# A two-layer graph network on one core: a support stage one pair deeper without GpSimd, two adj sums beside layer 0, z ahead of a low half

## What is computed

```python
h = jnp.maximum(_layernorm(x), 0.0)
# layer 0: quantised graph convolution
w_norm = (weight - mean) / std
weight_q = _weight_quant(w_norm, wgt_alpha, 3)      # round(|clip(w/alpha)| * 7) / 7 * sign * alpha
xq = _act_quant(h, act_alpha, 4)                    # round(min(h/alpha, 1) * 15) / 15 * alpha
support = relu(xq @ weight_q)
support_q = _act_quant(support, act_alpha2, 4)
x = x + adj @ support_q
# layer 1
h = jnp.maximum(_layernorm(x), 0.0)
S = (adj + adj.T) * 0.5 + I
dinv = where(deg > 0, deg ** -0.5, 0)               # deg = row sums of S
x = x + adj @ ((dinv[:, None] * S * dinv[None, :]) @ h)
```

## Time and profile before

| what | us |
|---|---|
| median of 3 runs (541.35 to 542.11) | 541.65 |
| the profiled execution, its own time | 541.03 |
| its span, first to last instruction | 538.9 |
| PE busy | 507.5 (94%) |
| DVE busy | 299.9 (56%) |
| ACT busy | 160.9 (30%) |
| POOL busy | 18.1 (3%) |

### The profile page before, as it was taken

One profiled execution on the slowest core, in us unless ns is written; L12 is line 12 of the kernel. 1 busy time (PEld: TensorE's weight loads), 2 busy tenths in 40 slices (PEclk: granted clock), 3 DMA queues, 4 the chain that ended last, 5 costly groups with the idle time before them and its releaser, 6 DMA issues.

```text
span 538.9 us, 6658 instructions
## 1 busy us (share of the span) xinstructions
PE 507.5 (94%) x2520; PEld 252.1 (47%) x2520; DVE 299.9 (56%) x415; ACT 160.9 (30%) x222; POOL 18.1 (3%) x24
## 2 busy tenths in 40 slices
PE   2868899999999979999998999999999999999997
PEld 2745455555555424444433444444444444444443
DVE  4996399997677996887789777743010010010001
ACT  0687576444444224434324212213000000000000
POOL 0134200000000000000000000000000000000000
PEclk9999999999999989999998999999999999999999
DMA  6970170254435132232322332204510000001001
GB/s 239 402 296 2 47 226 0 58 173 146 152 118 174 44 115 78 78 117 78 118 78 78 118 109 86 78 0 140 192 39 20 19 34 25 19 19 39 19 19 39
DMA packets 19251, 51.64 MB, mean 96 GB/s; under 512 B 2336, under 2 KB 2336, under 8 KB 19232
## 3 DMA queue, kind: packets, MB, share of 16 engines
q1 hardware_dynamic: 18656, 51.39, 28.2%
q10 hardware_dynamic: 576, 0.00, 0.1%
HBM read 42.99 MB, written 8.39 MB: 95 GB/s over the span
## 4 chain that ended last, share of the span: by engine, by line
PE 87%; DVE 8%; ACT 2%; DMA 2%; issue 1%; SPq 0%; ACTq 0%; DVEq 0%
PE ps_a L918 31%; PE ps_p L813 17%; PE ps_p L881 7%; PE ps_a L881 7%; PE ps_b L881 7%; PE ps_m L881 4%; PE ps_h L881 3%; PE ps_a L800 3%; PE ps_b L800 2%; PE ps_b L777 2%; DMA feat<-in_x 2%; DVE st L494 1%; DVE a_in L693 1%; DVE split L702 1%; DVE a_in L692 1%
## 5 line engine op out<-in xcount | busy, mean ns | idle before, releaser
L813 PE MATMUL ps_p<-small,at 128*128 128x512 f16 x448 | 101.6, 379 | 0.0
L749 DVE SCALAR_TENSOR_TENSOR feat<-ps_a,feat 128x512 f32<-128x512 f32 x16 | 11.1, 691 | 153.8 <-PE ps_a L918 153.8
L918 PE MATMUL ps_a<-a_in,at 128*128 128x512 f16 x384 | 85.5, 379 | 0.0
L918 PE MATMUL ps_a<-small,at 128*128 128x512 f16 x384 | 85.5, 379 | 0.0
L431 ACT ACTIVATE split<-a_in 128x1024 f16<-128x1024 f32 x32 | 33.8, 1057 | 113.8 <-PE ps_p L881 60.3
L813 PEld LDWEIGHTS ps_p<-small,at 128*128 128x128 f16 x448 | 43.7, 98 | 46.4 <-POOL small L306 0.3
L702 DVE TENSOR_TENSOR split<-a_in,split 128x1024 f16<-128x1024 f32 x32 | 39.2, 1224 | 36.7 <-ACT split L431 36.7
L918 PEld LDWEIGHTS ps_a<-small,at 128*128 (+1 forms) x384 | 37.5, 98 | 45.4
L918 PEld LDWEIGHTS ps_a<-a_in,at 128*128 (+1 forms) x384 | 37.5, 98 | 45.4
L881 PE MATMUL ps_a<-feat,split 128*128 (+1 forms) x180 | 45.0, 387 | 3.2 <-DVE small L706 3.2
L881 PE MATMUL ps_p<-feat,split 128*128 (+1 forms) x180 | 45.1, 388 | 0.0
(11 more groups left out here) (139 smaller groups left out, 466.9 us busy)
## 6 DMA issues: line engine op xcount, KB each, us to landing
a_in<-in_adj SPq DMA_DIRECT2D x48, 512.0 KB, 3.7
out<-feat SPq DMA_DIRECT2D x32, 256.0 KB, 2.0
feat<-in_x SPq DMA_DIRECT2D x8, 512.0 KB, 10.5
split<-in_adj SPq DMA_DIRECT2D x8, 512.0 KB, 5.3
at<-in_adj SPq DMA_DIRECT2D x8, 512.0 KB, 16.8
feat<-out SPq DMA_DIRECT2D x4, 1024.0 KB, 9.3
at<-in_L_gnn_weight SPq DMA_DIRECT2D x2, 512.0 KB, 5.9
scal<-in_L_gnn_act_alpha ACTq DMA_DIRECT2D x2, 0.5 KB, 6.9
```

What stands on the lines that cost most here:

```text
L749: nc.vector.scalar_tensor_tensor(xr, BANK[t % 2], 1.0 / (SA * SZ), xr, ALU.mult, ALU.add)\
L813: last = nc.tensor.matmul(l0_bank(r), at_block(r, lo, j), small[:, j * D:(j + 1) * D], start=(j == 0 and lo == 0), stop=(j == T - 1 and lo ...
L918: last = nc.tensor.matmul(BANK[n], at_block(t, lo, j), z_part(j, z_lo), start=(j == 0 and lo + z_lo == 0), stop=(j == T - 1 and lo == 1))
```

## The change

Support stage: PE transposes pair 1 before it multiplies pair 0, and so on, one pair deeper; the products of a pair go to one pair of banks, `ps_b` and `ps_a` in turn, and ACT evicts them in one operation. DVE rounds in one pass (adds the constant and subtracts it) straight to f16, and the clip of the support is a pass of its own on f16; POOL has no part any more. The quantised h is held negative and offset, so that ACT's eviction of the transposes can clip it. `GROUPS` gets one group more. Fewer `keep_warm` products. ACT evicts all transposes. Only units 0 and 1 are turned in the support stage, into `ps_p`, units 2 and 3 within row 0, and 4 to 11 in rows 1 to 3 (`TURNS`). In a later row the second turn comes after 8 products, not 16.

Boundary: adj units 0 and 1 of the sweep are loaded early into `split` and `tmp` and summed and split in rows 8 to 11 of layer 0. The statistics of rows 13 to 15 come as one group. The first sweep unit takes its banks in the order 0, 1, 2, 3, 6, 7, 4, 5. In the first sweep `sum_unit(v + 1)` stands ahead of `sum_lo(v)`. Between the sweeps seven of eight z halves stand ahead of the halves of unit 17.

```diff
-RING = 6
-EARLY = 6
-AHEAD = 14
+RING = 4
+AHEAD = 12
-GROUPS = (0, 2, 6, 10, T)
-LATE_GROUPS = (0, 13, 15, T)
+GROUPS = (0, 2, 4, 8, 12, T)
+LATE_GROUPS = (0, 13, T)
+LATE_SUMS = (0, 1, 2, 3)
...
         def turn_bank(u):
-            return ps_a if u < EARLY or u % 2 == 0 else ps_b
+            return ps_p if u < 2 else ps_b if u % 2 == 0 else ps_a
         def turn_before(u):
-            return u if u <= EARLY else u - 1
+            return 0 if u in (0, 2) else u - 1 if u > 3 else 1 if u == 1 else 0
...
         def sum_in(v):
-            k = SLOT[v % 4]
+            if v == 0:
+                return splitf[:, W:2 * W]
+            if v == 1:
+                return tmp[:, :]
+            k = (v - 2) % 4
             return a_in[:, k * W:(k + 1) * W]
...
+        TURNS = {r: [2 * r + 4, 2 * r + 5] for r in range(4, T - 2)}
+        TURNS.update({1: [4, 5, 6], 2: [7, 8], 3: [9, 10, 11]})
...
-            for u in range(AHEAD):
+            for n in range(4):
+                load_x(n)
+            rows(0)
+            rows(1)
+            for n in range(4, T // 2):
+                load_x(n)
+            for u in range(2, AHEAD):
                 rows(u)
+            sums(0)
+            sums(1)
...
             def copy_transposes(m):
...
-                nc.scalar.activation(hT[m % 2], hT_ps_bank[m % 2], ACT.Copy).then_inc(hT_ready, 1)
+                nc.scalar.activation(hT[m % 2], hT_ps_bank[m % 2], ACT.Relu, scale=-1.0).then_inc(hT_ready, 1)
             def scale_support(m):
-                for t in (2 * m, 2 * m + 1):
-                    act.wait_ge(sup_ps, t + 1)
...
+                nc.scalar.activation(sq[m % 2], sup_banks(m)[:, :], ACT.Relu, scale=c_sup).then_inc(sup_out, 1)
...
+            copy_transposes(1)
+            normalise(2)
+            scale_support(0)
+            hi_turned(0)
+            normalise(3)
+            copy_transposes(2)
+            group_root(3)
+            scale_support(1)
+            hi_turned(1)
+            copy_transposes(3)
+            for n in range(4, T // 2):
+                if n == 5:
+                    group_root(4)
+                normalise(n)
+                scale_support(n - 2)
+                copy_transposes(n)
...
             def quantise(n):
...
-                nc.vector.tensor_scalar(xq[n % 2], xq[n % 2], float(ACT_LEVELS), MAGIC, ALU.min, ALU.add)\
-                  .then_inc(xq_ready, 1)
+                nc.vector.tensor_scalar(hq[n % 2], xq[n % 2], -(MAGIC + ACT_LEVELS), MAGIC, ALU.add, ALU.add)\
+                  .then_inc(hq_ready, 1)
+            def round_support(m):
+                dve.wait_ge(sup_out, m + 1)
+                nc.vector.tensor_scalar(small[:, 2 * m * D:2 * (m + 1) * D], sq[m % 2], MAGIC, -MAGIC,
+                                        ALU.add, ALU.add).then_inc(sup_rounded, 1)
             def clip_support(m):
...
+                dve.wait_ge(sup_rounded, m + 1)
+                both = small[:, 2 * m * D:2 * (m + 1) * D]
+                nc.vector.tensor_scalar(both, both, float(ACT_LEVELS), None, ALU.min).then_inc(sq_ready, 1)
...
+            for r in range(1, 14):
+                now = TURNS[r]
+                turned_out(now[0])
+                x1_tile(r - 1)
+                for u in now[1:]:
+                    turned_out(u)
+                if r - 4 in LATE_SUMS:
+                    column_sum_late(r - 4)
+                if r == 8:
+                    sum_unit(0)
+                if r == 9:
+                    sum_lo(0)
+                if r == 10:
+                    sum_unit(1)
+                if r == 11:
+                    sum_lo(1)
...
             for v in range(3, T):
-                sum_unit(v)
+                if v + 1 < T:
+                    sum_unit(v + 1)
                 sum_lo(v)
-                if v + 1 < T:
-                    g_low(v + 1)
+                g_low(v)
             sum_unit(T)
             sum_unit(T + 1)
             sum_lo(T)
+            for t in range(B - 1):
+                z_lo(t)
             sum_lo(T + 1)
-            for t in range(B):
-                z_lo(t)
+            z_lo(B - 1)
...
-            keep_warm(26)
+            keep_warm(14)
             transpose_rows(0)
-            keep_warm(8)
+            keep_warm(4)
+            transpose_rows(1)
             pe.wait_ge(w_ready, 2)
             support(0)
...
-                for t in range(B):
+                for t in (0, 1, 2, 3, 6, 7, 4, 5) if first and h == 0 else range(B):
```

More of the change, by code:

```diff
@@ L57, in gnn_kernel @@
         tmp = sb("tmp", 2 * D)
-        junk = tmp[:, 0:D].bitcast(f16)
         ident = sb("ident", P, f16)
@@ L127, in gnn_kernel @@
         a_arr = [sem(f"a_arr{k}") for k in range(AHEAD)]
+        s_pre = [sem(f"s_pre{k}") for k in range(2)]
         s_arr = [sem(f"s_arr{k}") for k in range(4)]
@@ L360, in group_root @@
-            def group_root(g):
-                root(g + 1, GROUPS[g] + (g > 0), GROUPS[g + 1] + 1)
-            act.wait_ge(magic_set, 1)
-            group_root(0)
-            normalise(0)
-            act.wait_ge(c_wgt_ready, 1)
-            for h in range(2):
+                act.wait_ge(sup_ps, m + 1)
+                if m >= 2:
+                    act.wait_ge(sup_rounded, m - 1)
+                nc.scalar.activation(sq[m % 2], sup_banks(m)[:, :], ACT.Relu, scale=c_sup).then_inc(sup_out, 1)
@@ L614, in _ @@
             quantise(4)
[L615 to L618 removed]
+            round_support(2)
+            group_scale(4, [lambda: clip_support(2)])
+            for n in range(5, T // 2):
                 quantise(n)
[L620 to L624 removed]
@@ L625, in _ @@
-            clip_support(6)
-            clip_support(7)
+                round_support(n - 2)
+                clip_support(n - 2)
+            for m in range(T // 2 - 2, T // 2):
+                round_support(m)
+                clip_support(m)
+            lo_turned(2)
+            lo_turned(3)
             def x1_tile(r):
```

447 lines of the change are left out of this document (189 added, 258 removed).

## The result

| | before | changed kernel |
|---|---|---|
| median of the runs side by side, us | 541.88 (541.35 to 542.17, 4 runs) | 529.36 (528.62 to 530.4, 4 runs) |
| ratio of the times, 95% interval | | 0.9771 [0.9753, 0.979] |
| the profiled execution, its own time | 541.03 | 530.4 |
| its span | 538.9 | 528.6 |

A forecast was written before the change was run, and what follows sets the result against it. TensorE was taken to bound the kernel, idle only in the support stage, at the first sweep's start and at the turn of the sweeps. 541.03 - 7.3 - 4.0 + 2.0 = 531.7; median 0.6 above: 532.3 us, range 528.5 to 536.8.

The forecast's parts named there:

- The first sweep: Start of the first sweep: TensorE's wait for x1 of row 15 and its low clock go, 7.3 of 7.4 us gained.
- The turn of the sweeps: Between the sweeps: z follows each bank as it finishes, so 4.0 of 5.0 us lost there go.
- The start: Support stage up to row 0's end: 2.0 us lost, through VectorE's queue up to pair 1 and late roots.
- (a): Support stage, VectorE: unknown cost of an f16 to f16 pass in SBUF, taken as 0.69 us; lowest 0.2, 2.4 less in all.
- (b): Support stage: ScalarE's eviction over 1024 columns, between 1.02 and 2 x 0.78 us, taken as 1.0; later by 1.5 at most.
- (c): Support stage: TensorE's low clock after idling; 1.6 us less without it, up to 3 more if it falls back again.
- (d): Loads: two adj units and rearranged loads move 1 MB ahead of half of x; x still there well before its statistics.
- (e): ScalarE's row sums write 32 bits now; ScalarE is half idle there, so cost 0.
- A: Rival: the start gains or costs nothing, taken as -0.5, giving 529.8 us; chance 0.22.
- B: Rival: the start loses 5 us, low clock returning between pairs 2 and 5, giving 535.3 us; chance 0.14.
- C: Rival: at the boundaries VectorE reaches x1 too late, TensorE stops some 4 us and drops its clock, 538 us; chance 0.07.
- D: Rival: lower clock through the whole support stage, row 0 ending 15 us later than forecast, 547 us; chance 0.04.

The follow-up runs named there:

- sums_late: Changed kernel with adj units 0 and 1 summed and split behind the late sums at the end of layer 0, not beside rows 8 to 11: 537.85 us.
- pace: Changed kernel with adj unit v + 1 summed behind the low half and low g of unit v in the first sweep: 532.02 us.
- z_behind: Changed kernel with all z behind both halves of unit 17 again, on ScalarE and VectorE: 532.75 us.
- warm22: Changed kernel with 22 warming products instead of 4 between the transposes of pair 0 and pair 1, the first 14 kept: 527.98 us.
- loads: Changed kernel with the loads of adj units 0 and 1 behind all of x again: 529.33 us.
- roots: Changed kernel with ScalarE taking the roots of tiles 8 to 11 and 12 to 15 earlier, ahead of evictions: 527.88 us.
- first_early: Changed kernel with pair 0's support products ahead of the transposes of pair 1, behind 16 warming products: 528.39 us.
- roots_first: Changed kernel with the edits of roots and first_early together: 527.37 us.
- roots_warm22: Changed kernel with the edits of roots and warm22 together: 527.22 us.

## Why the prediction was right, and what it mis-sized

Forecast 532.3 us in a range of 528.5 to 536.8; measured 529.36, so 2.9 us too high. Only 1.3 us of that is in the steps (531.7 was forecast for the profiled execution, 530.4 is what it took). The other 1.6 is the step from the profiled execution to the median: 0.6 was added, as in the kernel before, where 1.0 had to be taken off. By its steps:

- **The first sweep, 7.3 of 7.4: right, in its size too.** 7.3 measured. The walk of VectorE's queue holds row by row: with L = 192.85, x1 of row 13 was expected to be done with its statistics by L-7.8 (184.54: L-8.3), adj unit 3 at L+0.9 (192.85: L), x1 of row 15 added by L+1.6 (193.80: L+0.95). sums_late shows that the two units beside layer 0 are needed: with them behind the late sums a wait for x1 and the low level return, 8.9 us, of which some 2 us are the buffer's. The order of the banks wasn't tested, but by the trace it wasn't needed: in the old order the bank of row 15 would be wanted 15 products of 0.216 us after L, at L+3.2, and x1 is there at L+0.95. Nor was the single late group tested; in the kernel before, its last group took 1.3 us of VectorE's queue ahead of x1 of row 15. pace shows that the other half of the step, a sum ahead of the low half, is needed too: without it 3 us are lost. The two add up to more than 7.3, since each is undone in a kernel in which the other stands.
- **The turn of the sweeps, 4.0 of 5.0: right.** 4.2 measured. Low z 7 was expected 10.5 us after the last unit's start (270.55), and is there after 10.3; the wait was expected at 0.8 and is 0.51, unit 18 at 0.25 late and is 0.18 late (286.95 - 281.59 - 5.18). z_behind gives 4.2 us back in the trace.
- **The start, 2.0 lost: right in sign and course, too large.** 1.16 measured. Forecast against trace, ends of the quantised pairs: 17.6 and 18.3; 24.4 and 24.65; 29.1 and 29.3; 37.3 and 37.0; 42.8 and 42.1; 47.2 and 46.2; 54.9 and 53.9 for pair 7. So the stage begins 0.7 later than forecast (x landed 0.6 later than in the trace of before, by chance) and gains 1.7 on the forecast from pair 0 to pair 5. Without the late x the start would have lost some 0.5 (an estimate: 1.16 less 0.6). **The mis-sized term is (a)**, the f16 to f16 passes of L525 and L516, taken at 0.69 us each: they take 0.41 and 0.42. Five of them lie in that stretch, which makes 1.4 of the 1.7 by their durations; no run has them slower, so this share is worked out, not measured. The Trainium skill, "VectorE: DVE Perf Modes", section "Side-by-side: where the cycles go for N=2048 bf16", from which the prediction had estimated 0.43, is borne out by these rows. The prediction gave both numbers and took the larger one; with 0.43 its sum would have been 1.3 lower, 531.0. Its bounds for the start, -1.5 to +4.5, are narrower than its own terms allow (2.0 - 2.4 - 1.6 to 2.0 + 1.5 + 3, so -2.0 to +6.5), and it doesn't say why; 1.16 lies in both.
- **The unknowns (b) to (e).** (b) ScalarE's eviction of 1024 columns takes 1.11, not 1.0, 0.3 later over three. (c) The low level came as expected: after a wait of 4.78 us the eight products take 3.62. It costs about 1 us: the distances of the six unchanged starts differ by 1.1 with its length, and warm22, without it, is 1.0 us faster. It came a second time, for pair 2's products (37.58, 3.49 us); the prediction had named that as its bound. The granted clock is 0.50 from 38 to 40 us and 0.59 in the microsecond behind, so by a hair this is also its own sign of being wrong, "a clock of 0.50 after 40 us". It cost little: its length doesn't order the distances (2.83 in loads with 53.4, 3.62 in pace with 53.3), and VectorE, which sets the pace there, stands only 0.19 us for the eviction behind it. Roots and first_early move that second fall to a later pair, and none of the edits takes it away. (d) is nothing that loads can tell. (e) shows in no wait.
- **The late roots** were forecast at 34.1 and 44.4 and came at 34.06 and 43.70; VectorE waited 1.19 and 0.98 us for them, and roots gives back 1.1 us of the median.
- **Rivals.** A (start at -0.5, 529.8) has the time nearest to the median, 0.4 us off where the forecast is 2.9 off, but not by its mechanism: in the trace the start loses 1.16. Its nearness is luck, and comes from the 1.6 us between profile and median: set against the profiled execution (530.4), its sum of 529.2 and the forecast's 531.7 are equally far off. B and C are out. D, the lower level through the whole support stage, is out: it came twice, the first time for one pair's products and the turn behind them, the second time for one pair's products. No run has transposes alone, so what the clock makes of them stays untested.

**What stays open.** The steps sum to 10.3 to 10.6 us in the traces, the medians differ by 12.5. The profiled execution of the changed kernel is the slowest of its four, 1.04 above its median, and that of before is 0.85 below its own; these two gaps are the difference. Two parts are seen. Over the twelve profiles of the changed kernel and its edits the first statistic of x starts between 9.71 and 10.82 us, and the start follows it; whether the executions without a profile have their x earlier wasn't measured. And the mean granted clock differs between executions of one kernel, and the time goes with it: the kernel before, run again on the three chips, took 540.3 to 540.7 us at 0.994, 541.1 to 542.1 at 0.990 or 0.991, and 542.8 to 543.2 at 0.987. The four runs of the changed kernel all have 0.990, so this doesn't explain their spread of 1.8 us.

## What to carry to other kernels

When the bounding engine stands at a boundary between stages, walk the helping engine's queue from the last point before the boundary: here two units moved to where VectorE had 5 us to spare in every 20 are worth some 7 us in the kernel as changed (an estimate: 8.9 measured, less some 2 through a shared buffer), though no operation became shorter. Whoever undoes such a step to measure it should look for buffers that the old order didn't share. In the one profile of that run 4.8 of the 6.6 us lost are waiting that the profile names. Ahead of an order that alternates two engines, look for the loop through both: 5.34 us a unit against 5.18, and the wait at the end of the sweep that grows out of it, cost 3 us. And fill an idle stretch that lowers the clock only as far as the next real work allows: 22 products between the transposes won about 1 us (likely, not proven), 26 ahead and 28 between them nothing.

## What the runs showed of the hardware that wasn't expected

- A VectorE pass from f16 to f16 in SBUF over 128x1024 takes 0.41 us, from f32 to f16 0.69.
- ScalarE's eviction of 128x1024 f32 from PSUM to f32 in one operation takes 1.11 us, against 2 x 0.78 in two of 128x512 before.
- A wait of some 2.73 us of TensorE in the support stage was followed by the low level for pair 2's products in the changed kernel (3.49 us) and in warm22 (3.40), and for pair 3's in roots (2.87); in first_early and sums_late waits of 2.74 and 2.73 ahead of pair 2's products were not (1.89 in both), and the next ones of 2.73 and 2.74 were (3.51 and 3.54). A wait of 3.17 was followed by the low level in roots_first (3.30) and not in first_early (1.89), and in roots_warm22 it followed one of 1.45 (3.10). The length of one wait doesn't decide it.
- Nor does it decide how long the low level lasts: behind the same wait of 4.78 us the same eight products took between 2.87 and 3.62 us in seven profiles.
- The arrival of x moves by 1.1 us over the twelve profiles; with the adj units behind it (loads, 10.69) it lies within the same span.
